# Adding the two half sums of a selective scan on GpSimd instead of by an identity product on TensorE

## The reference

```python
def step(state, inp):
    d, b, c, u = inp
    dA = jnp.exp(d[..., None] * A)
    state = state * dA + (d * u)[..., None] * b[:, None, :]
    y = jnp.einsum('bdn,bn->bd', state, c)
    return (state, y)
...
y = y + D[None, :, None] * x
y = y * silu(z)
```

## Time and profile before

| | |
|---|---|
| time, median of 3 runs | 1595.75 us (1594.79 to 1597.31) |
| span of the profiled execution, first to last instruction | 1594.7 us |
| PE busy | 1391.5 us (87%) |
| DVE busy | 936.9 us (59%) |
| POOL busy | 784.0 us (49%) |
| ACT busy | 709.8 us (45%) |

### The profile page before, as it was taken

One profiled execution on the slowest core, in us unless ns is written; L12 is line 12 of the kernel. 1 busy time (PEld: TensorE's weight loads), 2 busy tenths in 40 slices (PEclk: granted clock), 3 DMA queues, 4 the chain that ended last, 5 costly groups with the idle time before them and its releaser, 6 DMA issues.

```text
span 1594.7 us, 18873 instructions
## 1 busy us (share of the span) xinstructions
PE 1391.5 (87%) x6080; PEld 1030.4 (65%) x6080; DVE 936.9 (59%) x1186; ACT 709.8 (45%) x1303; POOL 784.0 (49%) x607
## 2 busy tenths in 40 slices
PE   6988983588899989897166999999999999999998
PEld 3535532566666656664166787878787887878786
DVE  2677767999999999998683224241414224241413
ACT  4445433266766776665143333333333333333332
POOL 0000000788888988885631445444544545444442
PEclk9898895699999999999555999999999999999999
DMA  3202214477977987863655900010000100010000
GB/s 105 108 26 81 107 53 165 158 240 257 315 257 234 319 269 264 281 198 125 218 198 203 364 14 0 0 66 1 14 0 13 52 13 0 0 53 0 0 0 26
DMA packets 78202, 191.29 MB, mean 120 GB/s; under 512 B 10856, under 2 KB 15752, under 8 KB 77120
## 3 DMA queue, kind: packets, MB, share of 16 engines
q1 hardware_dynamic: 64832, 157.03, 29.3%
q0 software_dynamic: 6400, 20.98, 4.1%
q10 hardware_dynamic: 6912, 12.59, 2.2%
HBM read 152.55 MB, written 38.01 MB: 119 GB/s over the span
## 4 chain that ended last, share of the span: by engine, by line
PE 58%; DVE 22%; issue 10%; ACT 4%; POOL 3%; DMA 3%; ACTq 0%; SPq 0%; DVEq 0%; POOLq 0%
PE decay L1675 22%; PE bank L1664 21%; DVE decay L1247 11%; DVE S L1256 4%; PE bank L1474 2%; PE decay L1430 2%; PE bank L1437 1%; DVE XH L1114 1%; PE bank L1494 1%; PE bank L1534 1%; PE decay L1484 1%; PE bank L1619 1%; POOL Y L767 1%; PE bank L1561 1%; PE decay L1480 1%
## 5 line engine op out<-in xcount | busy, mean ns | idle before, releaser
L1387 DVE CAST HFH<-HF 128x512 fp32r<-128x512 f32 x128 | 59.0, 461 | 496.7 <-ACT HF L1045 496.7
L815 POOL TENSOR_TENSOR W2L<-W2R,W2H 128x512 fp32r<-128x512 f32 x128 | 172.5, 1347 | 348.2 <-ACT W2H L1040 348.2
L728 POOL TENSOR_TENSOR S<-DTU,Bb 128x1024 f32<-128x1024 f32 x128 | 304.7, 2401 | 25.1 <-DVE row_hot L1229 21.7
L1247 DVE TENSOR_TENSOR_SCAN decay<-decay,S 128x1024 f32<-128x1024 f32 x128 | 292.9, 2288 | 0.5 <-ACT decay L892 0.5
L1664 PE MATMUL bank<-XSH,W1H 128*128 128x512 f32 x512 | 202.9, 396 | 4.2 <-POOL W1L L811 4.2
L1675 PE MATMUL decay<-W2H,HFH 128*128 128x512 f32 x512 | 200.4, 391 | 5.3 <-DVE HFL L1389 5.3
L1664 PE MATMUL bank<-XSH,W1L 128*128 128x512 f32 x512 | 203.0, 396 | 0.0
L1664 PE MATMUL bank<-XSL,W1H 128*128 128x512 f32 x512 | 202.3, 395 | 0.0
L1675 PE MATMUL decay<-W2L,HFH 128*128 128x512 f32 x512 | 199.9, 390 | 0.0
L1675 PE MATMUL decay<-W2H,HFL 128*128 128x512 f32 x512 | 199.7, 390 | 0.0
L811 POOL TENSOR_TENSOR W1L<-W1R,W1H 128x512 fp32r<-128x512 f32 x128 | 171.1, 1337 | 49.6 <-ACT W1H L1031 49.6
(11 more groups left out here) (212 smaller groups left out, 2102.3 us busy)
## 6 DMA issues: line engine op xcount, KB each, us to landing
WGU<-in_L_ffn_gate_w SPq DMA_DIRECT2D x48, 384.0 KB, 3.8
WGU<-in_L_ffn_up_w SPq DMA_DIRECT2D x48, 384.0 KB, 5.1
WD<-in_L_ffn_down_w SPq DMA_DIRECT2D x48, 384.0 KB, 4.9
Bb<-bc_rows SPq DMA_DIRECT2D x32, 512.0 KB, 7.9
Cb<-bc_rows SPq DMA_DIRECT2D x32, 512.0 KB, 9.7
expert_rows<-YT ACTq DMA_DIRECT2D x48, 256.0 KB, 4.2
W1R<-in_L_ffn_w SPq DMA_DIRECT2D x6, 1024.0 KB, 13.9
W2R<-in_L_ffn_w SPq DMA_DIRECT2D x6, 1024.0 KB, 14.1
```

Source lines behind the costliest of these rows:

```text
L728: pool.tensor_tensor(S[u % NP][:], DTU[:, ds(b, 1), c, :].to_broadcast([P, PAIR, L]), Bb[j][:], ALU.mult).then_inc(dbu_ready, 1)
L815: pool.tensor_tensor(W2L[f % 2][:], W2R[:, ds(e, 1), f, :].rearrange("p e d -> p (e d)"), W2H[f % 2][:].bitcast(F32), ALU.subtract).then_i ...
L1247: dve.tensor_tensor_scan(flat, flat, S[u % NP][:].rearrange("p i l -> p (i l)"), 0.0, ALU.mult, ALU.add).then_inc(scan_done, 1)
```

## The change

TensorE no longer adds the stored half; its transposing products of the last unit close the bank. ScalarE copies the half sum of half 1 over `DTU[:, b, c]` as before, and a new step `add_halves` on GpSimd adds `U[:, c]` to it in place. GpSimd does so at the end of its tile j for a group that ended in tile j - 2, after waiting for that group's `y_ready`; the groups that ended in tiles 46 and 47 follow after the loop. A new semaphore `halves_added` counts the additions. `load_u` waits for it instead of `s_summed`, and stands 4 units later in SyncE's order; `combine` waits for it on VectorE, and SyncE before the combining stage. GpSimd's own wait for all of `y_ready` before `gather_y` of sample 1 goes.

```diff
             def load_u(b, c):
                 if not isinstance(b, int) or b:
-                    sp.wait_ge(s_summed, b * UB + ((c + 1) * HP - UB // 2))
+                    sp.wait_ge(halves_added, (b - 1) * DC + c + 1)
...
-                        if (cuts[j - 1] if j else 0) < (b - 1) * UB + UB // 2 + (c + 2) * HP <= cuts[j]:
+                        if (cuts[j - 1] if j else 0) < (b - 1) * UB + UB // 2 + (c + 3) * HP <= cuts[j]:
                             load_u(b, c)
...
             sp.wait_ge(y_ready, B * GB)
+            sp.wait_ge(halves_added, B * DC)
...
+            def add_halves(b, c):
+
+                y = DTU[:, b, c, :]
+                pool.wait_ge(y_ready, b * GB + DC + c + 1)
+                pool.tensor_tensor(y, y, U[:, c, :], ALU.add).then_inc(halves_added, 1)
+
+            def ended(j):
+                return [(u // UB, u % UB // HP - DC) for u in units(j) if u % HP == HP - 1 and u % UB >= UB // 2] if j >= 0 else []
...
                 gate_by_up(j)
                 if j + 2 < SLOT_TILES:
                     gather(0, j + 2)
+                for b, c in ended(j - 2):
+                    add_halves(b, c)
+            for j in range(SLOT_TILES - 2, SLOT_TILES):
+                for b, c in ended(j):
+                    add_halves(b, c)
...
             gather_y(0, 0, 1)
             gather_y(0, 1, 2)
-            pool.wait_ge(y_ready, B * GB)
             gather_y(1, 0, 3)
...
+                dve.wait_ge(halves_added, (b + 1) * DC)
                 for t in range(T):
                     dve.wait_ge(gt_ready, b * T + (t + 1))
...
                         ins = pe.matmul(YS[:, t * P:(t + 1) * P], st[:, i, t * P:(t + 1) * P], ident[:],
-                                        start=(i0 + i + t == 0), stop=False, is_transpose=True, skip_group_check=True)
+                                        start=(i0 + i + t == 0), stop=(half == 1 and i0 == HP - 1 and i == PAIR - 1),
+                                        is_transpose=True, skip_group_check=True)
...
-                elif i0 == HP - 1:
-                    ins = pe.matmul(YS[:], ident[:], U[:, c, :], start=False, stop=True, skip_group_check=True)
                 ins.then_inc(s_summed, 1)
```

More of the change, by code:

```diff
@@ L351, in build_program @@
         y_ready = sem("y_ready")
+        halves_added = sem("halves_added")
         gu_loaded = [sem(f"gu_loaded{i}") for i in range(2)]
```

## The result

The changed kernel takes 1626.68 us (median of four runs, 1618.99 to 1627.18) against 1595.27 for the kernel before beside it: a ratio of 1.0183, interval 1.0163 to 1.0203. The profiled execution took 1627.18 us, with a span of 1625.5, 30.8 more than before.

What follows compares the result with a forecast made beforehand. VectorE was taken to bound the loop, and the chain through GpSimd's gathers the time after it. Stalls of 23.4 us plus 4.6 us of tail made 28.0 on 1595.75: 1624, own range 1614 to 1632, 8 in 10 within 1610 to 1640.

Steps and rivals of the forecast that it cites:

- The removed product: Sixteen products off TensorE, 0.86 us each, 13.8 us together: fifteen worth nothing, the sixteenth counting in the tail.
- The addition: Each addition of two 128 x 512 tiles on GpSimd takes 1.35 us; the sum holds six.
- The wait: GpSimd's wait for ScalarE's copy before an addition: costly for groups ending with a tile's last unit, otherwise nothing.
- The five stalls: In the loop, VectorE's `finish_h` waits for GpSimd's late gate: three times 5.62 us, twice 3.26 us, together 23.4 us.
- The ten other groups: Groups whose copy has just come; nine inside the loop, their 1.35 us additions covered by GpSimd's idle time: nothing.
- The tail: After the loop, the combining stage's gathers stand behind the last addition and begin 4.61 us later.
- The load of U: `load_u` comes one or two tiles later on SyncE; 0 to 0.4 us at the tightest place, taken as nothing.
- Rival 1: TensorE's clock falls after each loop stall and its work comes late: 8.5 to 17 us more, 1632 to 1641; chance 0.15.
- The lead of the products: GpSimd's products run ahead in the loop and hide the wait, leaving only the tail: 1600.4; chance 0.07.
- TensorE does not set the loop: Denies the rival that TensorE sets the loop, which gives back 13.8 us, tail taking 4.6: 1586.6; chance 0.03.

## Why the prediction was right, step by step

**The removed product.** Right that it is worth nothing in the loop, shown by the run without it. The 0.86 us that the last one gives in the tail are there too: with a product of zeros the change's tail is 0.87 us longer. What I had not seen is that the product also kept TensorE's clock up.

**The addition.** 1.28 us, taken as 1.35; six of them make 0.4 us too much. 1.35 is the mean of the earlier trace rows; the median of that row is 1.29.

**The wait.** The five stalls were forecast as 23.4 us and measured as 23.1. Shown from three sides: the waits alone, the tail's included, bring 24 us without additions, the additions alone bring none, and both together bring 4 when ScalarE's copy has come. The ten other groups cost nothing, as forecast. GpSimd's own waits were to be 4 to 6 us; they reach from 2.8 to 7.3, since it comes to each at another time, and the stalls do not depend on that.

**The tail.** Forecast 4.61, measured 4.61 in the profile. The steps are right; that it fits to the hundredth is luck, as the addition is 0.09 us shorter and the hand-overs that were left out come to about as much. As a cost of the order alone 4.61 is too much: the removed product delays the stored rows, so putting the order right gives back 2.4 us in the profile.

**The load of U.** No wait of ScalarE, as forecast. It stayed where the change has it in all variants of the change, down to those that take the time of before.

**The rivals.** The lead of the products hid nothing, as the gate stands behind them. TensorE does not set the loop. Rival 1 was right in kind and far too large. Its first half is there: in the 4.6 us behind the three long stalls the granted clock was 0.50, the 1.2 GHz level, and behind the two short ones 0.95 and 1.00. The first three of the five:

```profile
391.90:396.50 4.60, 4.55 (x9) 2.70 (x10) 4.57 (x4) 2.19 (x5) 4.58 (x3) 0.50 0.26 88
419.90:424.50 4.60, 4.60 (x16) 2.51 (x15) 4.50 (x4) 1.39 (x3) 4.58 (x3) 0.95 0.81 270
544.70:549.30 4.60, 4.52 (x9) 2.70 (x10) 4.50 (x4) 2.18 (x5) 4.58 (x3) 0.50 0.33 100
```

Its second half, a late next `finish_h`, is not: behind none of the stalls does the next one wait, as here behind the first. GpSimd is behind by then and leaves the gate room, which the prediction had held against this rival.

```profile
398.61 0.34 DVE L1277 SCALAR_TENSOR_TENSOR GU<-bank,GU 128x192 f32<-128x192 f32 x1
```

So its 8.5 to 17 us are not there. And the clock falls without stalls too: the variants without the product have 0.919 to 0.921, the waits alone with the product 0.917, the change with both 0.9145. The rival had one cause of two.

**The size.** 28.0 forecast, 30.8 in the span, 31.4 between the medians. The profile accounts for the span: 0.5 us more before the loop (the first `finish_h` of the loop comes that much later), 23.1 of stalls, 2.2 of other waits of `finish_h` (31.1 - 5.8 - 23.1), 4.6 of the tail, and 0.4 spread over the loop. The 2.2 are the part that was missed, and what makes them stays open. The clock is the likely cause, but single profiles do not show it: outside the five stalls `finish_h` waits 8.0 us in the change, 3.0 in the change with zeros, 9.7 with the waits alone, where the product is in place, and 5.8 before.

## What to carry to other kernels

In a queue in order, what an added wait costs is read from what stands behind it and from who waits for that: here 5.9 us of waiting cost 5.6 us of the engine that sets the pace, because its gate stood behind three products, while the same addition one tile later found the copy done and cost nothing. Ask at which step of its own order the producer gets to the awaited work, not when its inputs are there: the sum of u = 19 lay ready in PSUM for 5.6 us before ScalarE copied it. And before a product is taken off an engine that is not the bound, see what the engine's clock does when it has less to do.

## What the runs showed of the hardware that was not expected

Less work made TensorE slower. Without sixteen products of 0.86 us each the mean granted clock of the whole execution fell from 0.924 to between 0.919 and 0.921, and a product with zeros brought it back to 0.924. The Trainium skill, TensorE: Matmul & The Clock Gate, section "HAM oscillation — how this bites in real kernels", describes idle gaps in a kernel that set the clock back each time. The trace agrees in part: before the slow stretch at the end of the loop stand 2.41 us of idle time for 1.55, but in the kernel before 2.37 us of idle time are followed by products at full speed (752.38 in the earlier trace rows), so one pause's length alone does not decide it. Part 4 of the same page says that transposing products do not count as TensorE's activity in the same way; with them the mean clock came back half-way, 0.922, which neither bears that out nor contradicts it.

VectorE's addition of two tiles in SBUF went from 0.68 to 2.90 us beside GpSimd's products, which kept their 2.38 us.
